# A decoder layer's softplus in other places: the difference in SBUF behind the logarithm's sum, four PSUM places, and the feed-forward's first additions moved

## The reference

```python
    proj = hidden_states @ in_proj_w
    x, z = jnp.split(proj, 2, axis=-1)
    ...
    dt_r = rmsnorm(ssm_p[..., :R], dt_ln_w)
    ...
    dt = jnp.einsum('blr,dr->bdl', dt_r, dt_proj_w)
    dt = jax.nn.softplus(dt + dt_bias[None, :, None])
    ...
    ys = _selective_scan(xc, dt, A, Bm, Cm)
    ...
    g = linear_dsv3(xf, w1, w1_scale)
    u = linear_dsv3(xf, w3, w3_scale)
    h = jax.nn.silu(g) * u
    y = linear_dsv3(h, w2, w2_scale)
```

## Time and profile before

| | us |
|---|---|
| median of 3 runs | 3023.88 |
| lowest and highest | 3023.32, 3025.16 |
| the profiled execution | 3022.76 |
| its span, first to last instruction | 3021.4 |
| PE, DVE, ACT, POOL busy in it | 2817.7, 2384.0, 1571.1, 1816.3 |
| mean granted TensorE clock | 0.977 of 2.4 GHz |

### The profile page before, as it was taken

One profiled execution on the slowest core, in us unless ns is written; L12 is line 12 of the kernel. 1 busy time (PEld: TensorE's weight loads), 2 busy tenths in 40 slices (PEclk: granted clock), 3 DMA queues, 4 the chain that ended last, 5 costly groups with the idle time before them and its releaser, 6 DMA issues. The chain is left out here.

```text
span 3021.4 us, 35525 instructions
## 1 busy us (share of the span) xinstructions
PE 2817.7 (93%) x11950; PEld 2025.0 (67%) x11950; DVE 2384.0 (79%) x2206; ACT 1571.1 (52%) x2722; POOL 1816.3 (60%) x1068
## 2 busy tenths in 40 slices
PE   8995788888888989999999999999989999999998
PEld 7773344443222357988888888878768888887886
DVE  6678999999999958444777777765988888885677
ACT  4566455555664544215888888863433333334443
POOL 3475999999999932404888888851044444430034
PEclk9997899999989999999999999999999999999999
DMA  6357976666865653331111111225245555567654
GB/s 203 116 192 230 311 183 179 162 165 165 259 188 145 199 207 142 121 117 64 37 35 37 35 37 37 71 84 179 91 162 181 181 179 181 180 223 237 195 173 145
DMA packets 221698, 455.40 MB, mean 151 GB/s; under 512 B 34381, under 2 KB 48461, under 8 KB 219661
## 3 DMA queue, kind: packets, MB, share of 16 engines
q1 hardware_dynamic: 186094, 404.36, 43.1%
q10 hardware_dynamic: 35424, 48.77, 4.8%
HBM read 322.89 MB, written 130.15 MB: 150 GB/s over the span
## 5 line engine op out<-in xcount | busy, mean ns | idle before, releaser
L2151 POOL TENSOR_TENSOR at_p_lo<-at_p,at_p_hi 128x512 fp32r<-128x512 f32 x384 | 515.8, 1352 | 241.0 <-ACT at_p_hi L2044 233.7
L937 POOL TENSOR_TENSOR scan_dbx<-scan_u,scan_b_bc 128x1024 f32<-128x1024 f32 x256 | 596.6, 2366 | 0.0
L1109 ACT ACTIVATE mamba_ps<-scan_dt,scan_a_neg 128x512 f32<-128x512 f32 (+1 forms) x512 | 332.0, 680 | 312.4 <-DVE scan_g L1127 287.4
L1138 DVE TENSOR_TENSOR_SCAN mamba_ps<-mamba_ps,scan_dbx 128x1024 f32<-128x1024 f32 x195 | 439.9, 2283 | 4.8 <-ACT mamba_ps L1111 2.8
L3036 POOL TENSOR_TENSOR ff_raw<-ff_raw,ff_scale 128x512 f32<-128x512 f32 x112 | 116.4, 1072 | 359.5 <-DMA ff_raw<-in_w 251.0
L2071 DVE TENSOR_REDUCE at_neg_max<-heads_ps 128x1 fp32r<-128x1536 f32 x128 | 224.9, 1757 | 134.3 <-PE heads_ps L2163 132.4
L108 PE MATMUL heads_ps<-ff_x_hi,ff_w_hi 128*128 128x512 f32 x784 | 309.6, 395 | 17.2 <-DVE ff_u L2796 7.2
L109 PE MATMUL heads_ps<-ff_x_lo,ff_w_hi 128*128 128x512 f32 x784 | 307.8, 393 | 0.0
L110 PE MATMUL heads_ps<-ff_x_hi,ff_w_lo 128*128 128x512 f32 x784 | 307.4, 392 | 0.0
L2040 ACT ACTIVATE at_p<-heads_ps 128x512 f32<-128x512 f32 x384 | 228.5, 595 | 109.8 <-PE heads_ps L2187 95.7
L2044 ACT ACTIVATE at_p_hi<-at_p 128x512 fp32r<-128x512 f32 x384 | 242.8, 632 | 12.2
(11 more groups left out here) (303 smaller groups left out, 6973.5 us busy)
## 6 DMA issues: line engine op xcount, KB each, us to landing
scan_dt<-dt SPq DMA_DIRECT2D x128, 256.0 KB, 4.8
scan_u<-u SPq DMA_DIRECT2D x128, 256.0 KB, 7.5
ff_raw<-in_w SPq DMA_DIRECT2D x56, 512.0 KB, 4.4
ff_down_ar<-ac SPq DMA_DIRECT2D x98, 256.0 KB, 2.9
ff_down_hr<-hc SPq DMA_DIRECT2D x98, 256.0 KB, 2.7
in_w<-in_w_in SPq DMA_DIRECT2D x36, 512.0 KB, 3.8
ff_act_w<-in_w SPq DMA_DIRECT2D x14, 1024.0 KB, 7.1
hc<-ff_act_t SPq DMA_DIRECT2D x56, 256.0 KB, 6.2
```

The source lines that it names most:

```text
L937: nc.gpsimd.tensor_tensor(dbx[n % SL][:].rearrange("p (h l) -> p h l", h=2), u[it % 2][:, c:c + 2], b_bc[b][:, k // 2].unsqueeze(1).to_bro ...
L1109: nc.scalar.activation(at[:, h * L + h:(h + 1) * L], dt[it % 2][:, c, h:L], ACT.Exp, scale=a_neg[:, it % IT, e:e + 1]).then_inc(a_ready, 1)
L1138: nc.vector.tensor_tensor_scan(out[:], ps_a[n % SA], dbx[n % SL][:], 0.0, ALU.mult, ALU.add).then_inc(scanned, 1)
L2151: nc.gpsimd.tensor_tensor(p_lo[n % NSL][:], p[n % NSL][:], f32(p_hi[n % NSL][:]), ALU.subtract).then_inc(p_lo_done, 1)
```

## The change

In `mamba_in`, for groups 8 to 15: `remainder` is cut into `parts` ((1 + e) - 1) and `remainder` (the difference). Both now write `dd[i]` in SBUF, for all groups. The ramp with the logarithm is written over v in `ps_x[i]`, and the total adds it to `dd[i]`. The order on DVE is parts, ramp, remainder, total; `place_free` stands ahead of parts. `ps_t` is gone, and its banks are a fourth place: `ps_x` of groups 8 to 15 begin at banks 4, 6, 2, 4, 6, 2, 0, 4. A product now waits for `dt_done` of the group three (13 and before) or four ahead in place of `r_done`; the last gate tile lies in bank 1 and comes behind group 11's product, with group 12's product inside it; ACT copies it out behind the logarithm of group 13; SP's stores of group 12 and of this tile stand behind the load of the scan's second dt. The scan's first exponentials wait for `dt_done`.

In the feed-forward, `add_u2(0)`, `add_u2(1)`, `add_12(0)`, `add_12(1)`, `add_22(0)`, the SiLUs (0,5), (0,3) and the products (1,5), (1,3) stand among the first remainders and no longer in the loop over `order`; weight 11 is rounded one place earlier; the tiles h lie in SBUF behind the v tiles, and the first SiLUs wait for fewer x remainders and one store.

```diff
-    main_bank = [ps_all[:, n % 2] for n in range(NT - 1)] + [ps_all[:, 0]]
+    main_bank = [ps_all[:, n % 2] for n in range(NT - 1)] + [ps_all[:, 1]]
...
-    ps_x += [ps_all[:, m:m + 2] for m in (6, 4, 0, 6, 4, 0, 6, 4)]
+    ps_x += [ps_all[:, m:m + 2] for m in (4, 6, 2, 4, 6, 2, 0, 4)]
...
-        for i in range(BG + 3, BG + 5):
-            store_dt(i)
-        store_gate(3)
+        store_dt(BG + 3)
         sp.wait_ge(main_done, NT)
         scan.load_dt(sp, 1)
+        store_dt(BG + 4)
+        store_gate(3)
...
-            if i == BG + 4:
-                gate(act, 3)
             exponentials(i + 1)
             logarithm(i)
...
             logarithm(i + 1)
...
+            if i == BG + 4:
+                gate(act, 3)
...
+        def parts(i):
+            place_free(i)
+            dve.wait_ge(e_done, i + 1)
+            nc.vector.tensor_scalar(dd[i][:], ee[i % 2][:], 1.0, -1.0, ALU.add, ALU.add).then_inc(t_done, 1)
...
-            r = dd[i] if i >= IN_PSUM else ll[i % 2]
-            nc.vector.scalar_tensor_tensor(r[:], ps_x[i], 0.0, ll[i % 2][:], ALU.max, ALU.add).then_inc(r_done, 1)
+            r = ps_x[i] if i >= IN_PSUM else ll[i % 2][:]
+            nc.vector.scalar_tensor_tensor(r, ps_x[i], 0.0, ll[i % 2][:], ALU.max, ALU.add).then_inc(r_done, 1)
...
-            c = ps_t if i >= IN_PSUM else ll[i % 2][:]
-            nc.vector.tensor_tensor(dd[i][:], dd[i][:], c, ALU.add).then_inc(dt_done, 1)
+            r = ps_x[i] if i >= IN_PSUM else ll[i % 2][:]
+            nc.vector.tensor_tensor(dd[i][:], dd[i][:], r, ALU.add).then_inc(dt_done, 1)
...
         for i in range(IN_PSUM, NG):
+            parts(i)
+            ramp(i)
             remainder(i)
-            ramp(i)
             total(i)
...
                 if i == BG + 2:
-                    pe.wait_ge(left, NF - 1)
+                    pe.wait_ge(r_done, BG)
+                elif i < BG + 6:
+                    pe.wait_ge(dt_done, i - 2)
+                elif i == BG + 6:
+                    pe.wait_ge(left, NF)
                 else:
-                    pe.wait_ge(r_done, i - 2)
-                if i == BG + 5:
-                    pe.wait_ge(left, NF)
+                    pe.wait_ge(dt_done, BG + 4)
...
-        for i in range(BG + 2, NG):
-            if i == BG + 5:
-                main(pe, NT - 1)
+        for i in range(BG + 2, BG + 4):
+            dt_product(i)
+        main(pe, NT - 1, lambda: dt_product(BG + 4), 4)
+        for i in range(BG + 5, NG):
             dt_product(i)
...
-                act.wait_ge(before.r_done, IT - 2 + n)
+                act.wait_ge(before.dt_done, IT - 1 + n // 2)
...
-                act.wait_ge(x_lo_done, len(pieces))
-                for s in x_st:
-                    act.wait_ge(s, 16)
+                act.wait_ge(x_lo_done, piece[3, HK - 1] + 1)
+                act.wait_ge(xt_done, 3 * HK)
+                act.wait_ge(x_st[2], 16)
...
         rest_w(10)
+        rest_w(11)
         for h in range(2):
-            add_11(h)
+            add_u2(h)
+        add_11(0)
         dve.wait_ge(x_st[1], 16)
         sum_x(4, x(1, 1), x(0, 1))
-        add_u2(0)
+        add_11(1)
+        add_12(0)
         rest_x(4)
-        rest_w(11)
         sum_x(6, x(1, 0), x(0, 0))
-        add_u2(1)
+        add_12(1)
+        product(1, 5, 0, sg11_done, c11_done, h11_done)
         rest_x(6)
         rest_w(12)
         rest_w(13)
+        add_22(0)
+        product(1, 3, 1, sg12_done, c12_done, h12_done)
```

More of the change, by code:

```diff
@@ L614, in vector @@
                 total(i + 1)
+        parts(BG - 2)
         remainder(BG - 2)
@@ L617, in vector @@
         normalize(1)
+        parts(BG - 1)
         remainder(BG - 1)
@@ L2318, in attention_out_feed_forward @@
     act_at = Arena(nc, "ff_act", sb.at)
-    hb, tt = ([act_at(f"{n}{i}", [P, L]) for i in range(4)] for n in ("h", "t"))
     w2 = act_at("w2", [P, 2, H])
-    v = [act_at(f"v{i}", [P, L]) for i in range(4)]
+    tt = [act_at(f"t{i}", [P, L]) for i in range(4)]
+    v, hb = [], []
+    for i in range(4):
+        v.append(act_at(f"v{i}", [P, L]))
+        hb.append(act_at(f"h{i}", [P, L]))
     y = sb("y", [P, HT, TOK])
@@ L2694, in scalar @@
         round_w(10)
+        round_w(11)
         round_x(4, t_ready)
-        round_w(11)
+        silu(0, 5, 0, c11_done, sg11_done)
         round_x(6, t_ready)
+        silu(0, 3, 1, c12_done, sg12_done)
         round_w(12)
@@ L2708, in scalar @@
             if h % 2 == 0:
-                if q == 3:
+                if q == 3 and h:
                     silu(h, 3, 1, c12_done, sg12_done)
@@ L2712, in scalar @@
                     silu(h, 1, 3, c22_done, sg22_done)
-                elif q == 5:
+                elif q == 5 and h:
                     silu(h, 5, 0, c11_done, sg11_done)
@@ L2962, in vector @@
                 add_u2(h)
-            elif q == 3:
+            elif q == 3 and j:
                 add_12(h)
@@ L2967, in vector @@
             elif q == 4:
-                add_22(h)
+                if h:
+                    add_22(h)
                 if up:
@@ L2973, in vector @@
                     sum_h(j, 2, hb[3], hb[1])
-            elif q == 5:
-                if j:
-                    add_11(h)
+            elif q == 5 and j:
+                add_11(h)
                 if up:
```

15 lines of the change are left out of this document (1 added, 14 removed).

## The result

The changed kernel takes 3028.62 us (median of 20 runs, 3024.89 to 3030.34), the kernel before 3023.70 (20 runs, 3020.22 to 3026.45). The ratio is 1.0015, with a 95% interval of 1.0009 to 1.0021: about 4.5 us slower. The forecast was 3030.4, from 3020.0 to 3033.5, and 6.5 us slower. The difference is real but lies within the 0.2% that counted there as the same.

A forecast was written before the change was run, and what follows sets the result against it. In the projection tail no engine is full and a chain through several engines sets the end; the feed-forward's steady part is TensorE-bound. 3023.88 before, with +5.8 (scan start) and +0.7 (feed-forward), gave 3030.4 us, range 3020 to 3033.5.

The forecast's parts named there:

- The start of the scan: End of the projection tail: first scan at 298.6 against 292.78 before, +5.8 us.
- walk: Projection tail, groups 8 to 15 followed step by step through the engines with row durations, to the first scan at 298.6.
- Logarithm 10 14.9 later: Projection tail: POOL's weight remainder and product hold group 9's operations, so logarithm 10 ends at 262.8, 14.9 after 247.9.
- The pair of 12.3: Projection tail: the round trip from logarithm to logarithm, two groups, takes 12.3 us instead of 9.95.
- The gate copy that makes the third pair 13.3: Projection tail: group 14's product waits for ACT's gate copy behind logarithm 13, so logarithm 14 ends at 288.4.
- Exclusion in every second group: Projection tail: DVE's difference meets POOL's product in SBUF, taking about 2.4 to 2.5 us in every second group.
- Rival A: Projection tail: POOL's product starts while DVE reads PSUM, sparing the difference; scan at 292.2, sum 3024.0, not slower; chance 0.18.
- What exclusion costs: Projection tail: without DVE and POOL excluding each other in SBUF a pair takes 11.2 us and the scan starts at 292.2.
- The later difference: Projection tail: the difference now comes behind the logarithm's sum, and group i+2's absolute value waits for it; part of 12.3.
- The feed-forward: Feed-forward start: early products gain 9.3 us, but product 15 waits for a late bank and TensorE restarts slowly; +0.7 us.
- Rival B: Feed-forward: product 15's bank isn't late and TensorE keeps the 9.3 us won; sum 3020.4; chance 0.05.
- rival D: Both places: POOL wins each SBUF tie (+7) and the late bank drags product 17; +9.5, 3033.5 and over; chance 0.12.

The follow-up runs named there:

- e1: The changed kernel with the feed-forward of the kernel before, so the projection's edits alone; 3027.50 us, ratio 1.0016 to before.
- e5: The changed kernel with ACT's copy of the last gate tile put back between the exponentials of groups 12 and 13; 3025.25 us, ratio 1.0009 to before.
- e2: The changed kernel with the projection of the kernel before, so the feed-forward's edits alone; 3024.09 us, ratio 1.0003 to before.
- e3: The changed kernel with GpSimd's products of groups 8 to 13 made on 8 of each 512 columns only; 3025.38 us, ratio 1.0010 to before.
- e12: The changed kernel with the edits of e3 and e5 together; executed once, not timed, first scan 59.62 us behind the start of the last reciprocal.
- e8: The changed kernel with only the difference ahead of the logarithm's sum again; executed once, not timed, first scan 63.01 us behind the start of the last reciprocal.
- e6: The changed kernel with the edits of e8 and e5, and GpSimd's products of groups 8 to 13 behind the next difference; 3019.67 us, ratio 0.9991 to before.
- e10: e6 with the feed-forward of the kernel before, no other edit; 3018.54 us, ratio 0.9986 to before.

## Why the prediction came out as it did

**The start of the scan: right, 1.2 to 2.0 us too late.** Forecast was 298.6, or 64.8 behind the mark; the changed projection has 62.75 to 63.60. The walk's steps, one by one:

- *Logarithm 8 at 247.93*: 247.95, and the first operation of group 8 does wait for the landing of the store (3.27 us of idle time).
- *Logarithm 10 14.9 later*: 13.38 to 14.21 in six executions. This is the step that was too large. Five of them have 14.2, with the clash that I described: in e1 POOL's remainder, issued at 250.54, takes 3.34 us, the first operation of group 9 takes 1.52 and its difference 2.23, ending at 257.72 where I had 258.3. In the profiled execution of the changed kernel the clock was at its lower level (0.52 from 240 to 245 us), the copy ahead of the remainder and so the remainder came late (253.21, behind the start of that operation), the clash with it fell away, and the pair took 13.38.
- *The pair of 12.3*: 12.17 and 12.18.
- *The gate copy that makes the third pair 13.3* (288.4 - 275.1): 13.26, and e5 took it away.
- *10.2 from logarithm 14 to the scan*: 9.84.
- *Exclusion in every second group*: 2.23 or 2.24 in the odd groups, where 2.4 to 2.5 was forecast. Rival A, that the product starts beside a PSUM operation and spares the difference, is out: no difference of an odd group was spared.

What the sum was compared with was also off. The scan of before starts at 58.96 in its trace, and at 61.27 in e2 with the same code. Against the mean of the two the cost is 3.3, not 5.8: 1.2 of the difference come from this ground, and 1.3 from the walk. A single execution of before was taken as the ground, and it was a good one.

**What exclusion costs: right in a pair, not tested in the sum.** A pair without it was put at 11.2, and e3 and e12 have 11.15. The whole walk without it was put at 292.2, so 6.4 us earlier. e3, with the products of groups 8 to 13 made small, gave 1.2 to 2.1; the second pair lost 1.03, as said, and the third nothing, because of the copy. Without the late copy too, e12 gave 3.1 to 4.0. But both runs left the rest of POOL's work whole: the products of groups 6, 7 and 14, the weight remainder and the products for the scan. Beside these the first operation of group 8 still took 1.79 us in e12, the difference of group 9 2.25 and that of group 15 2.23. So the mechanism and the price of a pair were right, and whether 6.4 is right for the whole no run shows.

**The later difference: it costs only where exclusion and the copy do not hold the pair.** I named both, the difference behind the logarithm's sum and exclusion, as what makes the pair 12.3. e8 put the difference back alone and won nothing: with exclusion on, either place costs the same. With exclusion and the late copy gone, the third pair takes 11.15 with the difference late (e12) and 8.95 with it early (e6), so there the place is worth 2.2.

The rule cited from the Trainium skill (SBUF — State Buffer, section Who interferes with whom), that the two engines hold each other off for a whole instruction, holds in the tails of all these traces: a difference that was issued while POOL worked ended 1.08 or 1.09 us behind POOL, and the operations that read PSUM took their 1.22 or 1.23 beside it. It holds for the operation with one SBUF input too, which the rule counts only in its two-port mode (no row says which mode it ran in): in e3 the first operation of group 8, usually 0.68 us, was issued at 246.93 and took 1.97, to the end of POOL's two products (242.70 to 248.34) and 0.56 more.

**The feed-forward: right in each step, and nothing in the sum.** The early products came as said: product 11, (0,6), 9.3 us early (39.82 in place of 49.11). Product 15 was to start 1.3 early after about 8 us of idle time: it started 1.8 early after 7.50. The restart at 1.2 GHz was to cost 2.0: from product 15 to 20 it is 15.37 in place of 13.60, so 1.8. The sum was +0.7, measured -0.05 between the two traces and 1.0003 in e2; the two differences, 0.5 and 0.2, are all of it. That the clash with POOL's scaling of w2 would stay was right (2.93 us, before 2.34). Rival B is out, and so is the drag on product 17 in rival D: TensorE does not wait before it.

**The sum.** +5.8 and +0.7 against some 3.3 and 0 from the marks, and 4.5 us from the timed runs (2.7 to 6.3). The direction and the size were right, and the forecast put itself just outside the 0.2% edge when the time came to lie just inside. That the timed 4.5 lies nearer to the forecast than the 3.3 from the marks is no merit of the walk: the marks' means come from few executions, and the timed interval reaches down to 2.7.

## What to carry to other kernels

Before moving a vector operation from PSUM to SBUF, look at what GpSimd does at that moment: 0.55 us was saved on each of eight operations, and each odd difference and each product paid 1.0 and 0.4 us for it; letting GpSimd's product wait for the next difference, with two more moves, gave 6.4 to 7.3 us at the scan's start in e6 and 2.0 more in e10. When one cause is taken away and little is gained, take away the second as well before giving the first up: e3 and e5 alone looked small (1.2 to 2.1 and 0.3 to 1.1), together they made 3.1 to 4.0. And a place that an engine wins early in a saturated stage is worth only as much as the latest of all chains that feed it: 7.5 us won at product 15 were gone at product 21.
